# Scatters to DRAM tables in a graph network kernel: written plainly in place of added

## The reference

```python
# layer 0, twice (l = 0, 1): attention over edges
scores = einsum('ehd,ehd->eh', q[dst], k[src]) * scale
attn = softmax of scores over the edges of one dst
h = h + segment_sum(attn * v[src], dst) @ wo[l] + bo[l]
h = h + gelu(layernorm(h) @ w1[l] + b1[l]) @ w2[l] + b2[l]
# layer 1: edges grouped by source
e = exp(leaky_relu(el[src] + er[dst]))
out = segment_sum(e / rowsum[src] * x[dst], src)
# layer 2: four hops over the edges; layer 3: messages along the edges, summed at dst
```

## Time and profile before

| | |
|---|---|
| time, median of 3 runs | 5620.3 us (5606.59 to 5629.95) |
| span of the profiled execution | 5234.5 us |
| median of the runs less this span | 385.8 us |
| POOL busy | 3710.0 us (71%) |
| PE busy | 3992.0 us (76%) |
| mean granted clock of PE | 0.891 of full speed |

### The profile page before, as it was taken

One profiled execution on the slowest core, in us unless ns is written; L12 is line 12 of the kernel. 1 busy time (PEld: TensorE's weight loads), 2 busy tenths in 40 slices (PEclk: granted clock), 3 DMA queues, 4 the chain that ended last, 5 costly groups with the idle time before them and its releaser, 6 DMA issues.

```text
span 5234.5 us, 64530 instructions
## 1 busy us (share of the span) xinstructions
PE 3992.0 (76%) x17691; PEld 3086.9 (59%) x17691; DVE 2746.1 (52%) x6371; ACT 1847.6 (35%) x5458; POOL 3710.0 (71%) x3085
## 2 busy tenths in 40 slices
PE   4565554667985655699796777789999999988886
PEld 3443343445664433466464444468888888877886
DVE  6476667885436555888532888850010002235555
ACT  1154444663334444577232222120000000046665
POOL 4477778888887777888888777788888800037775
PEclk8878777998987777799897888889999999989998
DMA  8699995663339999576423777746666655557676
GB/s 261 200 328 334 329 324 131 161 161 45 31 56 338 338 337 312 132 168 144 75 21 54 208 211 207 178 89 154 153 141 139 149 152 151 153 146 198 198 200 164
DMA packets 734961, 951.33 MB, mean 182 GB/s; under 512 B 277381, under 2 KB 526260, under 8 KB 734472
## 3 DMA queue, kind: packets, MB, share of 16 engines
q1 hardware_dynamic: 419634, 538.30, 34.0%
q0 software_dynamic: 298192, 385.84, 31.5%
q10 hardware_dynamic: 16774, 23.00, 1.2%
HBM read 727.03 MB, written 219.80 MB: 181 GB/s over the span
## 4 chain that ended last, share of the span: by engine, by line
POOL 36%; PE 23%; issue 19%; DMA 16%; SPq 3%; DVE 2%; POOLq 0%; ACT 0%; DVEq 0%
POOL arena L863 24%; PE bank L2443 21%; POOL ATT L900 6%; POOL sc L886 6%; DMA sc<-arena 4%; DMA ATT<-arena 4%; DMA VE<-arena 4%; DMA arena<-KVT,arena 3%; SPq L574 2%; DMA arena<-X1T,arena 1%; PE bank L2152 1%; SPq L570 1%; PE bank L2477 1%; DVE arena L1027 0%; PE bank L2428 0%
## 5 line engine op out<-in xcount | busy, mean ns | idle before, releaser
L2443 PE MATMUL bank<-arena 128*128 128x256 f32 x5000 | 1101.8, 380 | 1.7 <-DVE arena L1686 1.2
L2443 PEld LDWEIGHTS bank<-arena 128*128 128x128 f32 x5000 | 945.5, 190 | 131.4 <-DVE arena L1686 2.0
L863 POOL DMA_INDIRECT arena<-KVT,arena x832 | 808.6, 972 | 278.2 <-issue 239.9
L2287 PE MATMUL bank<-arena 128*128 128x264 f32 x1664 | 606.0, 529 | 453.8 <-ACT arena L1892 439.4
L863 POOL DMA_INDIRECT arena<-YT,arena x416 | 422.9, 1017 | 568.6 <-DMA YT<-arena 442.1
L2287 PEld LDWEIGHTS bank<-arena 128*128 128x128 f32 x1664 | 419.8, 264 | 639.3 <-issue 546.8
L916 POOL DMA_INDIRECT arena<-ATTR,arena x416 | 655.4, 1575 | 144.9 <-issue 144.9
L900 POOL DMA_INDIRECT ATT<-arena x391 | 642.0, 1642 | 130.6 <-issue 110.6
L886 POOL DMA_INDIRECT sc<-arena x391 | 642.5, 1643 | 123.8 <-issue 111.9
L2244 PE MATMUL bank<-arena 128*128 128x273 f32 x1664 | 455.3, 412 | 141.1 <-DVE arena L1406 117.9
L863 POOL DMA_INDIRECT arena<-X1T,arena x416 | 420.4, 1011 | 126.9 <-issue 123.2
(11 more groups left out here) (309 smaller groups left out, 5462.0 us busy)
## 6 DMA issues: line engine op xcount, KB each, us to landing
VE<-arena SPq DMA_DIRECT2D x208, 512.0 KB, 5.8
arena<-VE SPq DMA_DIRECT2D x208, 512.0 KB, 3.6
arena<-ATT SPq DMA_DIRECT2D x250, 320.0 KB, 3.0
arena<-AM SPq DMA_DIRECT2D x250, 320.0 KB, 2.9
ATT<-arena POOLq DMA_DIRECT2D x25, 1600.0 KB, 6.6
arena<-LOCT SPq DMA_DIRECT2D x312, 128.0 KB, 5.4
arena<-ATT SPq DMA_DIRECT2D x75, 384.0 KB, 4.3
AM<-arena SPq DMA_DIRECT2D x100, 256.0 KB
```

The source lines that it names most:

```text
L863: GP.indirect_dma_start(out=ring[:, i % n, k, :], out_offset=None, in_=table, in_offset=bass.IndirectOffsetOnAxis(ap=idx[:, 4 * i + k:4 * ...
L2287: mm = P.matmul(b_[:, 0:264], OHQ[:, i % 3, k * 128:(k + 1) * 128], QS[:, i % 4, k, :], start=True, stop=True)
L2443: mm = P.matmul(bank[j][:, 0:256], left[:, 128 * j:128 * (j + 1)], right[:, u, :], start=(u == 0), stop=(u == W - 1))
```

## The change

In the scatters of the order by source the operand `compute_op=ALU.add` is dropped: each DMA writes its 128 rows over what the table holds, in place of adding to it. Indices, values, tables, semaphores and the clearing of the tables stay. The other two lines with `compute_op` on this path, 900 and 916, stay as they are.

```diff
@@ -885,8 +885,7 @@
                         GP.wait_ge(*ordered[k](c // KS))
                     GP.indirect_dma_start(
                         out=tg3[k], out_offset=bass.IndirectOffsetOnAxis(ap=poss[:, c:c + 1], axis=0),
-                        in_=code[:, c:c + 2], in_offset=None, bounds_check=R2 + 127,
-                        compute_op=ALU.add).then_inc(ordered[k].sem, 16)
+                        in_=code[:, c:c + 2], in_offset=None, bounds_check=R2 + 127).then_inc(ordered[k].sem, 16)
```

## The result

| | median | runs | ratio to the kernel before, 95% |
|---|---|---|---|
| kernel before | 5620.08 us | 5606.59 to 5629.95 (4) | |
| changed kernel | 6020.24 us | 6013.60 to 6026.65 (4) | 1.0707 [1.0690, 1.0723] |

I had forecast 5615 us, in a range from 5595 to 5632 us. The change costs 400 us. The profiled execution of the changed kernel took 6015.14 us, with a span of 6014.0 us, so 1.1 us lie outside the span. Lines behind the scatter are one lower than in before (L1244 is the old L1245, L2243 the old L2244).

The account below looks back on a forecast made before the run. POOL's queue of indirect DMAs was taken to bound the middle; its saved 239 us become a wait for KVT except 5.4 us, so 5620.3 - 5.4 = 5614.9, rounded to 5615 us, range 5595 to 5632 us.

Parts of the forecast that it names:

- The cost of a plain scatter: Scatter stage L886: 0.95 us each in place of 1.56, saving POOL 239 us; stage 534 us long.
- The scans' five still scatters: Scatter stage: four scatters and part of a fifth stand still during DVE's scans, most of 33 us, kept unchanged.
- rival 3: Scatter stage: plain scatters land later and the wait on their own table paces it; slower, 5650 us; chance 0.05.
- The wait for KVT that takes over: Head of gather k1: POOL waits for layer 1's K and V rows, 225 us, leaving 5 to 6 us gained; 0.78.
- The other working of this gain, 6.4 us: Start of gather k1: table there at 1551.6 us, from the last KVT write's issue plus a 2.3 us landing.
- my -5.4: Start of gather k1: 5.4 us earlier, at SP's first LOCT load (1552.6 against 1557.98 us), passed on to the end.
- the port's share: DVE in mix0: less hold-up by POOL's scatters, 7 ns on each of 285 instructions, 2 us.
- 6.7 of the 9 us of a possible gain: PE in mix0: L2152 at 388 ns in place of 406, 6.7 us more; gain bounded at 9 us.
- the 28 us that it would have given mix0: DVE in mix0: if POOL fully blocks it, 0.1 us for each of 285 instructions; rival 2, chance 0.07.
- Denser scatters raise the load in v0: Stage v0: denser scatters load the DMA engines more, still below gather k1's 0.99; cost put at nothing.
- my 0.86: Stage v0: DMA engines' busy share with the denser scatters, up from 0.70.
- the profile gives no total for that execution: Whole kernel: median 385.8 us above the profiled span of 5234.5 us, taken as outside the span and untouched.

Follow-up runs that it names:

- e4_every4: Changed kernel with one POOL memset and its wait behind every fourth plain scatter: 5623.15 us, against 5625.51 us for the kernel before.
- e7_rows64: Changed kernel with each plain scatter writing only 64 of its 128 rows, on the chip where the kernel before takes 5239.48 us: 5272.10 us.
- e7_every2: Changed kernel with one POOL memset and its wait behind every second plain scatter: 5232.44 us, ratio 0.9985 to the kernel before.
- e0_before: The kernel before, unchanged, run and profiled once more: 5661.64 us against 5659.26 us, ratio 1.0007.

## Why the prediction was wrong

**Right.** The cost of a plain scatter (0.95 us taken, 0.98 measured; the stage 553 us long where I had 534). The scans' five still scatters (7.68, 6.68, 6.73, 6.93 and 3.42 us in the timeline; each DMA stands until the scan is over, as before). Its landing didn't pace the stage: 8.5 us of waits for sc in all, so rival 3 had the sign and not the mechanism. The wait for KVT that takes over, and its size: the earlier trace rows put the scatters 5.4 us late against SP's first load, and from v0's end to gather k1 it was 357 us in before and 350 to 352 us in the runs in which POOL waited for KVT, save e4_every4 with 356. (The other working of this gain, 6.4 us, added the 0.38 us of the issue to a landing that is counted from its start; it gives 6.8.) Around that point in the changed kernel:

```profile
2049.18 0.38 ACTq L1825 DMA_DIRECT2D KVT<-arena  x1
...
2052.83 2.71 SPq L588 DMA_DIRECT2D arena<-LOCT  x6
2053.03 0.99 POOL L863 DMA_INDIRECT arena<-KVT,arena  x1 [601.05 <-DMA KVT<-arena]
```

POOL starts 0.2 us after SP, where it was 5.4 us behind. On the quick chip, with the scatters paced, this is what is left: -7.0 us at 0.9985 [0.9976, 0.9994], against my -5.4. There the wait for KVT is 214.8 us where the stream is dense (e7_rows64). The engines beside POOL didn't change speed for it (the port's share): L2151 takes 406 ns with POOL idle, as beside its scatters, and L1163 takes 426 ns against 433. So PE's 388 ns in qkv0, from which I took 6.7 of the 9 us of a possible gain, had another reason than POOL's scatters. The Trainium skill's rule of the port pair (SBUF — State Buffer, "Who interferes with whom") holds for the scans here; the 28 us that it would have given mix0 at its word didn't come.

```profile
L2151 PE MATMUL bank<-arena 128*128 128x256 f32 x108 | 26.9, 406 | 0.9 <-ACT arena L1952 0.9
...
L1163 DVE TENSOR_TENSOR arena<-arena 128x256 f32<-128x256 f32 x9 | 3.8, 426 | 3.8 <-ACT arena L1821 3.7
```

**The step that failed** is "Denser scatters raise the load in v0 ... I cost it at nothing". I looked for the harm of a denser stream in the DMA engines' share and in the port between DVE and POOL, and neither was it (the share is 0.10 in the slow stretch, and 0.47 beside a v0 that isn't slow, in e7_rows64, in place of my 0.86). It came where no row of the page shows a load: on the chips on which the times were taken, PE's signals to ACT and DVE arrive 16 us late as long as POOL issues indirect DMAs, of either direction and with 64 or 128 rows, 1.41 us or less apart on the mean, and not at 1.64 us. At that pace v0's chain, which goes PE, ACT and DVE, PE once a group, takes 22 us a group in place of 3.3: 374 of the 400 us. The rest are the groups before and behind that stretch (54 us for 47 and 246 us for 285 of the instructions, which at 0.83 us are 39 and 236 us: 25 us more). Adding was the brake: at 1.56 us and 0.30 us of issue its scatters come 1.86 us apart, slower than that limit.

**The second step that failed** is "the profile gives no total for that execution ... 385.8 us more, and the change touches nothing outside the span". The 386 us weren't outside. The profile of before was of an execution like those of the quick chip (5239.48 us; gathers k0, k1 and l1 of e7_every2 take 536, 522 and 547 us), and the times were of a chip like that of e0_before, on which signals are late in the gather stages, where POOL's own pace is 1.25 us a DMA. Had I read the 386 us as work of the kernel that the profile didn't show, I would have had to ask which stage holds it, and what a denser queue does there. On such a chip the gathers, by their own waits for DVE, slow down to 1.52 us apart; the scatters wait for nobody but their own landings, and don't.

**Open.** What makes PE's signals late isn't shown. The runs exclude the direction, the rows of each DMA (64 or 128), the stage and VE's loads; they leave the number of POOL's indirect DMAs per us, with their waits and increments, on certain chips. The sum of all increments isn't the measure: v0 of e4_every4 has 17.1 per us and isn't slow, while the last gather stage, with 13.6 per us in the first profile, is 74 us longer in e0_before. That the lateness climbs and then stands at 16 us, with 128 rows or 64, looks like a queue that is full; no run shows one. One rival is untested: that the recording itself makes the signals late. Every run, timed ones too, has a span and a clock, so each was recorded, and the lateness comes only where records are lost. No run shows the kernel unrecorded. What distinguishes the quick chip isn't known, nor was the changed kernel itself run there. The half-row kernel at 1.40 us a scatter ran there with v0 at 339 us and took 765 us more on the other, of which 381 us are the difference that the kernel before shows between the two. That speaks for a changed kernel that is about as quick as before on the quick chip; it was not measured. Nor can these records tell a late signal from a last matmul that ends late, since the ends of matmuls are modelled; the 16 us lie somewhere between its start and the recorded increment.

## What to carry to other kernels

A queue that gets faster and then waits can still cost: ask not only what its transfers collide with, but whether it was the slow pace of its DMAs that kept the engines' signals prompt. Here a pause behind every 2nd scatter took the loss away: 0.15% faster than before on one chip, and level with it (0.2% faster, single runs) on another, where the change without pauses cost 7%. When the profiled span and the measured time differ by 7%, the profile is of another kind of execution, and the difference is the first thing to place. A remedy for late signals must be timed on both kinds of chip: with both pauses the kernel was 0.6% faster than before on one, and pauses in the gathers alone cost 3.2% on another.

## What the runs showed of the hardware

- An engine's signal can arrive 16 us after its work, again and again by nearly the same time, while PE starts 2.3 us after ACT and DVE and POOL waits 8.5 us in all for the landings of its scatters. The view that shows it is a wait on "remote" of 20 us on an engine whose releaser has long been done; where records are missing, the same wait is called "issue". In e0_before PE too has waits on "remote" (L2287: 19 of them, up to 6.6 us), so in the gather stages other signals than PE's may be late as well.
- On these chips the limit lies between 1.64 us (v0 341 us) and 1.41 us (706 us) between indirect DMAs of POOL, by their mean beside v0; gathers of 8-byte rows at 1.33 us pass it as well (742 us).
- A trace can lack a good part of its semaphore records (of before, 92,806 in the first profile and 50,870 in e0_before), and its list of waits then blames the wrong releaser.
- Chips differ: the same kernel took 5239 us on one and 5621 to 5659 us on four others. Between the two profiles of before (5234.5 and 5663.4 us) 399 of the 429 us lie in the four gather stages.
- By the page's list of queues the change took 43,792 packets from POOL's queue, 298,192 to 254,400: that is 391 scatters with 112 packets fewer each, so a plain scatter's 128 rows of 8 bytes leave in 16 packets, and the adding one's in 128. The packet records bear it out: 6,256 packets of 64 bytes in the one, 50,048 of 8 bytes in the other.
